# Weighted sums of a four-layer kernel: final products in quarters between the chunks, expansions in halves, and four batches in a loop body

## The chip, the cores and the metric

The kernel runs on one core of one Trainium2 chip. The metric is device time in microseconds (us) for one execution of the whole program. Five engines work side by side: TensorE (PE in the profile, with its weight loads as PEld), VectorE (DVE), ScalarE (ACT), GpSimd (POOL) and SyncE (SP), which here only issues transfers. Each works through its own instructions in order; they meet through semaphores.

## The reference, cut to what matters

Three attention layers run over 32 batches of 128 x 1024 numbers, and a fourth layer then aggregates over nearest neighbours. Only the last step of that fourth layer is touched:

```python
idx = _knn(x_loc, k)                     # k = 30 nearest of 1024 points
...
att = jax.nn.softmax(h[..., 0], axis=-1) # 1024 x 30 weights for each of 32 batches
xk = x.transpose(0, 2, 1)[bidx, idx]     # gathered rows
agg = jnp.einsum('bnkc,bnk->bnc', xk, att)
return x + agg.transpose(0, 2, 1)
```

So for each batch and each of 1024 points, 30 rows of 128 numbers are picked by index, weighted and summed, and `x` is added.

## The kernel before, in words

The kernel has four stages one behind the other: the attention layers and neighbour search over all batches (to about 5200 us), a small network with batch norms, the softmax, and the **weighted sums**, which is the stage of this change. It begins at about 5838 us and ends with the program.

In the weighted sums the gather is made into matrix products. A point's index is split into a low part l (0 to 15) and a high part h (0 to 63). For every batch `i`:

- **normalise** (DVE, line 1973) makes the attention weights of the batch; two **transposes** (PE, line 1111, tile TP) turn them.
- **weights** (DVE, line 1985, 16 instructions for each half of the batch) spread the turned weights over the 16 values of l, into BA (tile S for half 0, pd for half 1).
- **blocks** (ACT, line 1564, four instructions for each of four groups `v`), which this text calls expansions, spread BA into block form BD. There are two buffers of BD, one for even and one for odd `v`.
- **onehots** (DVE, line 1994, one instruction for each of eight chunks `c`) compare the high parts with 0 to 63, into A1 (tile gat, two buffers).
- **chunk** (PE, line 1124, 32 matmuls, each shown twice in the trace) multiplies A1 by BD into SCA (even `c`) or SCB (odd `c`). One BD serves two chunks.
- **columns** (ACT, line 1572, one instruction for each chunk) copy that result out into WT (two halves).
- **final** (PE, line 1137, 32 matmuls for each half, in pairs on PD and MISC that run together), the final product of WT with the table of rows X3D. The product of half 0 (the early one) needs chunks 0 to 3, that of half 1 (the late one) chunks 4 to 7. The late one is made inside the next batch's turn.
- **finish** (DVE, line 2008, two instructions), which the change calls the sums, adds `x` to both halves and lets the store go.

SP issues for each batch the store of the result, the load of the index table, of X3D and of `x`; these wait for finish. POOL splits the indices (lines 631 to 635).

The waits that matter: a chunk needs its one-hots, its BD, and the columns of the chunk two before it. The one-hots of chunk `c` need chunk `c - 2` done (buffer). The columns need their chunk. Expansions of `v` need both chunks of `v - 2` done. The early product needs finish of the batch before, since both products share the tiles PD and MISC. The order on each engine is written out by hand:

```python
# PE                                      # DVE                       # ACT, for v in range(4)
chunk 0, chunk 1                          normalise(i + 1)            blocks v + 1 (or 0 of i + 1)
final(i - 1, ..., 1)                      onehots 0, 1                columns 2v
transposes(i + 1)                         weights(i, 1)               columns 2v + 1
chunks 2 to 5                             onehots 2, 3
final(i, ..., 0)                          finish(i - 1)
chunks 6, 7                               onehots 4, 5
                                          weights(i + 1, 0)
                                          onehots 6, 7
```

PE and DVE run batch 0 as straight code, then a loop (`Fori`) of 15 passes with two batches in its body, then batch 31. ACT loops over 31 batches, one in its body. The loop bodies have 714 instructions on PE (a matmul counted once), 145 on DVE and 43 on ACT.

Of the kernel before, what the change touches and what calls it, by code (L numbers as in the profile page):

```python
# [31 lines left out]
def program(nc, x_in, ctx_in, mask_in, w_in, b_qkv, w_out, wq, wk, wv, wo, at, bq, bk, bv, bo,  # L32
            mlp_k, consts, out, NB=B):
# [16 lines left out]
    with stack:  # L50
# [195 lines left out]
        LV, HV = 16, 64  # L246
# [36 lines left out]
        def settle(eng):  # L283

            eng.sem_inc(waited, 1)
# [357 lines left out]
        def _(pe):  # L643
# [497 lines left out]

            def aggregate(i, par, k, first=False, last=False):
                chunk(i, 0)
                chunk(i, 1)
                if not first:
                    final(i - 1, 1 - par, k - 1 + par, 1)
                if not last:
                    transposes(i + 1, 1 - par)
                for c in range(2, 6):
                    chunk(i, c)  # L1150
                final(i, par, k, 0)
                chunk(i, 6)
                chunk(i, 7)
                if last:
                    final(i, par, k, 1)
# [13 lines left out]
        def _(act):  # L1169
# [388 lines left out]
            def blocks(i, v):  # L1558
                half, w = v // 2, v % 2
                act.wait_ge(ba_done, i * 2 + half + 5)  # L1560
                act.wait_ge(chunk_ready, i * 8 + 2 * v + 2)
                src = BA[half].rearrange("r (h p) l -> r h p l", h=2)[:, :, 32 * w:32 * w + 32, :]
                for j in range(4):
                    last = A(BD[v % 2][:, :, :, j, :], src, ACT.Copy, scale=blockmask[0:GROWS, j:j + 1])
                last.then_inc(bd_done, 1)
# [20 lines left out]
            blocks(0, 0)  # L1586
            with act.Fori(0, NB - 1) as i:
                aggregate(i)
# [4 lines left out]
        def _(dve):  # L1593
# [417 lines left out]
            def aggregate(i, par, k, first=False, last=False):  # L2011
# [26 lines left out]
            with dve.Fori(0, NB // 2 - 1) as pair:  # L2038
                for odd in (1, 0):
                    aggregate(pair * 2 + (2 - odd), odd, pair + (1 - odd))  # L2040
# [86 lines left out]
```

## Time and profile before

| | |
|---|---|
| time, median of 3 runs | 7017.76 us (6999.0 to 7027.35) |
| profiled execution, its own time | 6984.93 us |
| its span, first to last instruction | 6983.1 us |
| first chunk of the weighted sums | 5849.73 us |
| mean granted TensorE clock | 0.950 |
| PE busy over the whole span | 89% |
| DVE busy over the whole span | 87% |

The profile is of one execution. Its time exceeds its span by 1.8 us, and it is 32.8 us under the median of the runs, so a sum made on the trace is carried over to the median as a difference. Times of instructions below are microseconds from the start of the span. A bracket at the end of a row gives the idle time of that engine before the row and what ended it; "issue" means that nothing seen in the profile was waited for.

### The profile page before, as it was taken

The numbers are of one execution on the slowest core, as the hardware profiler recorded it, in microseconds if no ns is written. First come the engines' busy times: TensorE is split into PE (matmuls) and PEld (weight loads), VectorE is DVE, ScalarE is ACT, GpSimd is POOL, SyncE is SP. The second block draws the span as 40 slices with busy tenths as digits, with TensorE's granted clock in tenths as the row PEclk, the third lists the DMA queues.
The fourth block names the chain that finished last, engine by engine and source line by source line (L and its number), as shares of the span: only waits on it lengthen the run. The fifth ranks groups of instructions, "written<-read, shape, count | busy, mean of one in ns | idle before, by whom it ended". The sixth has DMA issues, their size and how long they took to land.

```text
span 6983.1 us, 208271 instructions
## 1 busy us (share of the span) xinstructions
PE 6195.4 (89%) x79430; PEld 4459.4 (64%) x79430; DVE 6047.0 (87%) x8509; ACT 4321.9 (62%) x10325; POOL 2693.2 (39%) x3399
## 2 busy tenths in 40 slices
PE   8999999999999999999999999999995795888888
PEld 4666666666666666666666666666664234888878
DVE  6999999989999999999999999999996578777776
ACT  4666666666666666666666666666662156666666
POOL 2444444454444444444444454444443101111110
PEclk9999999999999999999999999999997898999999
DMA  3222222222222222222222222222224003222222
GB/s 118 76 75 72 71 71 68 69 75 80 76 72 78 72 68 68 72 75 76 71 72 68 69 72 83 72 75 75 75 70 133 21 16 76 63 64 62 64 66 59
DMA packets 301388, 499.32 MB, mean 72 GB/s; under 512 B 103859, under 2 KB 217699, under 8 KB 299683
## 3 DMA queue, kind: packets, MB, share of 16 engines
q1 hardware_dynamic: 246733, 389.60, 18.3%
q10 hardware_dynamic: 53589, 95.21, 4.3%
q8 instruction: 706, 11.57, 0.7%
q14 instruction: 360, 2.94, 0.1%
HBM read 410.45 MB, written 74.30 MB: 69 GB/s over the span
## 4 chain that ended last, share of the span: by engine, by line
DVE 41%; PE 29%; issue 21%; DMA 5%; ACT 2%; DVEq 1%; SPq 0%; POOL 0%; ACTq 0%; POOLq 0%
DVE pd L1680 10%; DVE m L1670 9%; DVE idx L1676 8%; PE SCA L901 7%; PE PD L1137 6%; DVE mx L1692 4%; PE SCA L1124 3%; DMA gat<-low_scratch 3%; DVE gat L1624 3%; PE SCB L1124 3%; DVE gat L1994 2%; PE SCB L733 2%; PE SCA L1042 1%; PE SCB L1042 1%; PE TP L1050 1%
## 5 line engine op out<-in xcount | busy, mean ns | idle before, releaser
L1670 DVE MAX8 m<-pd 128x8 f32<-128x1024 f32 x1024 | 1244.3, 1220 | 154.5 <-issue 72.1
L1676 DVE FIND_INDEX8 idx<-m,pd 128x8 uint32<-128x1024 f32 x1024 | 1245.2, 1218 | 0.0
L529 POOL TENSOR_TENSOR prod<-prod,hm 128x480 f32<-128x480 f32 x384 | 396.2, 1032 | 1934.8 <-ACT prod L1310 1923.9
L1680 DVE MATCH_REPLACE8 pd<-m,pd 128x1024 f32<-128x1024 f32 x768 | 928.2, 1209 | 0.4
L1192 ACT ACTIVATE pd<-PD,xxcol 128x512 f32<-128x512 f32 x514 | 368.7, 717 | 722.3 <-PE PD L684 692.3
L708 PEld LDWEIGHTS MISC<-ptab,gat 128*128 128x128 bf16 x23400 | 642.3, 96 | 177.7 <-DVE gat L1624 87.7
L1994 DVE TENSOR_TENSOR gat<-maskT,con 120x2048 f32<-120x2048 f32 x256 | 584.0, 2322 | 166.8 <-PE SCA L1124 164.9
L708 PE MATMUL MISC<-ptab,gat 128*128 128x24 bf16 x23400 | 653.2, 174 | 80.8 <-DVE gat L1624 78.3
L1290 ACT ACTIVATE S<-SCA,mx 128x64 f32<-128x64 f32 (+1 forms) x2560 | 590.1, 406 | 118.7 <-DVE mx L1692 118.3
L1290 ACT ACTIVATE S<-SCB,mx 128x64 f32<-128x64 f32 (+1 forms) x2560 | 580.4, 387 | 19.9 <-DVE mx L1692 19.9
L683 PE MATMUL PD<-arena 128*128 128x512 f32 x1028 | 552.6, 619 | 33.0 <-ACT pd L1192 28.3
L1624 DVE TENSOR_SCALAR gat<-gat,con 128x2560 bf16<-128x2560 bf16 x396 | 427.7, 1086 | 82.6 <-DMA gat<-low_scratch 82.6
L631 POOL TENSOR_SCALAR maskT<-ctxT 120x256 f32<-120x256 f32 x32 | 12.9, 404 | 1241.1 <-DVE gat L1994 895.9
L797 PE MATMUL PD<-reg,arena 128*128 128x128 f32 x4096 | 488.1, 277 | 0.0
L901 PE MATMUL SCA<-arena,OT 128*128 128x512 f32 x1024 | 484.9, 634 | 0.0
L797 PEld LDWEIGHTS PD<-reg,arena 128*128 128x128 f32 x4096 | 467.1, 192 | 15.1 <-issue 12.3
L1243 ACT ACTIVATE kexp<-reg,con 128x256 f32<-128x256 f32 x1024 | 435.0, 521 | 10.8 <-PE SCA L833 8.7
L578 POOL TENSOR_SCALAR hm<-hif 128x240 bf16<-128x240 f32 x256 | 396.6, 1700 | 8.0
L872 PEld LDWEIGHTS TP<-reg,ET 128*64 128x64 f32 x8192 | 279.1, 137 | 179.2 <-issue 178.3
L1124 PE MATMUL SCA<-arena,gat 120*64 120x64 f32 x8192 | 281.4, 230 | 109.4 <-DVE gat L1994 81.6
L872 PE MATMUL TP<-reg,ET 128*64 128x34 f32 x8192 | 326.0, 226 | 57.8 <-DVE on L1704 56.9
L901 PEld LDWEIGHTS SCA<-arena,OT 128*128 128x128 f32 x1024 | 207.7, 207 | 251.4 <-issue 251.4
(272 smaller groups left out, 14188.3 us busy)
## 6 DMA issues: line engine op xcount, KB each, us to landing
gat<-low_scratch SPq DMA_DIRECT2D x396, 640.0 KB, 3.9
arena<-in_ctx ACTq DMA_DIRECT2D x33, 512.0 KB, 4.2
x_scratch<-arena ACTq DMA_DIRECT2D x33, 512.0 KB, 3.2
x3T_scratch<-reg ACTq DMA_DIRECT2D x33, 512.0 KB, 3.4
maskT<-in_mask SPq DMA_DIRECT2D x32, 512.0 KB
arena<-in_x ACTq DMA_DIRECT2D x32, 512.0 KB, 4.4
reg<-in_ctx ACTq DMA_DIRECT2D x32, 512.0 KB, 3.5
arena<-x3T_scratch SPq DMA_DIRECT2D x32, 512.0 KB, 6.0
```

What stands on the lines that cost most here:

```text
L683: mm(PD[:, :], ctx[:, t * P:(t + 1) * P], ctx[:, h * 512:(h + 1) * 512], start=True, stop=False)
L708: last = mm(place[:, o:o + 3 * NT], oh[n % NOH][:, kk * 256 + half * P:kk * 256 + (half + 1) * P], ptab[:, part, :, :].rearrange("p t c -> ...
L797: last = mm(PD[:, c % 2 * P:(c % 2 + 1) * P], Wq[:, kc, c * P:(c + 1) * P], hT[:, kc, :], start=(kc == 0), stop=(kc == KC - 1))
L872: last = mm(TP[64 * half:64 * half + 64, (4 * b + pair) * 2 * VW:(4 * b + pair + 1) * 2 * VW], ET[:, o:o + 64], V2[:, (4 * g + 2 * b + hal ...
L901: last = mm(SC[0][:, h * 512:(h + 1) * 512], OT[:, c * P:(c + 1) * P], Wo[:, c, h * 512:(h + 1) * 512], start=(c == 0), stop=(c == KC - 1))
L1124: last = mm(SC[c % 2][64 * h:64 * h + 64, p * 64:(p + 1) * 64], A1[c % 2][:, h, p, :], BD[v % 2][:, h, c % 2 * 16 + p, :, :].rearrange("r ...
L1290: last = A(S[g][:, r * keys:(r + 1) * keys], SC[g][:, r * keys:(r + 1) * keys], ACT.Exp, bias=mx[g][:, r:r + 1])
L1624: V.tensor_scalar(oh[n % NOH], oh[n % NOH], iota_p, None, ALU.is_equal).then_inc(oh_done, 1)
L1670: V.max(m, buf[:, :]).then_inc(found, 1)
L1676: last = V.max_index(idx[:, t, 8 * r:8 * r + 8], m, buf[:, :])
L1680: V.match_replace(buf[:, :], m, buf[:, :], -3.0e38).then_inc(found, 1)
L1994: V.tensor_tensor(A1[c % 2], low[:, :, 16 * part:16 * part + 16].unsqueeze(3) .broadcast_to([GROWS, 2, 16, HV]), iota64[0:GROWS, :].unsque ...
```

## The change

On PE each final product is cut into four quarters (four values of l each, 16 pieces in two lines of tiles), which are put between the chunks. On DVE finish goes from behind the fourth one-hots to behind the fifth, and weights of both halves each move earlier or later by a place. On ACT the expansions may be cut in halves, and only those of `v = 3` are really parted, by the columns of chunk 4; the expansions for the next batch stand behind the columns of chunk 5 instead of before those of chunk 6. All loops get four batches in their body: PE and DVE 7 passes over batches 2 to 29, ACT 7 passes over batches 0 to 27. The bodies then have 1426 instructions on PE, 285 on DVE and 163 on ACT. No computation is added or left out.

```diff
-            def final(i, par, k, half):
-                pe.wait_ge(wt_done, i * 8 + 4 * half + 6)
-                if half == 0:
-                    pe.wait_ge(x3T_ld[par], k * 32 + 32)
-                    pe.wait_ge(out_done, i + 2)
-                settle(pe)
-                for l in range(LV):
+            def final(i, par, k, half, piece):
+                if piece == 0:
+                    pe.wait_ge(wt_done, i * 8 + 4 * half + 6)
+                    if half == 0:
+                        pe.wait_ge(x3T_ld[par], k * 32 + 32)
+                        pe.wait_ge(out_done, i + 2)
+                    settle(pe)
+                for l in range(4 * piece, 4 * piece + 4):
...
-                last.then_inc(fin_ready, 1)
+                if piece == 3:
+                    last.then_inc(fin_ready, 1)
...
                 chunk(i, 0)
+                late(0)
+                late(1)
                 chunk(i, 1)
-                if not first:
-                    final(i - 1, 1 - par, k - 1 + par, 1)
+                chunk(i, 2)
+                late(2)
                 if not last:
                     transposes(i + 1, 1 - par)
-                for c in range(2, 6):
-                    chunk(i, c)
-                final(i, par, k, 0)
+                late(3)
+                chunk(i, 3)
+                chunk(i, 4)
+                final(i, par, k, 0, 0)
+                final(i, par, k, 0, 1)
+                chunk(i, 5)
                 chunk(i, 6)
+                final(i, par, k, 0, 2)
+                final(i, par, k, 0, 3)
                 chunk(i, 7)
...
-            with pe.Fori(0, NB // 2 - 1) as pair:
-                for odd in (1, 0):
-                    aggregate(pair * 2 + (2 - odd), odd, pair + (1 - odd))
+            aggregate(1, 1, 0)
+            with pe.Fori(0, (NB - 4) // 4) as four:
+                for u in range(4):
+                    aggregate(four * 4 + 2 + u, u % 2, four * 2 + 1 + u // 2)
+            aggregate(NB - 2, 0, NB // 2 - 1)
...
             def aggregate(i, last=False):
-                for v in range(4):
-                    if v < 3:
-                        blocks(i, v + 1)
-                    elif not last:
-                        blocks(i + 1, 0)
-                    columns(i, 2 * v)
-                    columns(i, 2 * v + 1)
+                for v in (1, 2):
+                    blocks(i, v, 0)
+                    blocks(i, v, 1)
+                    columns(i, 2 * v - 2)
+                    columns(i, 2 * v - 1)
+                blocks(i, 3, 0)
+                columns(i, 4)
+                blocks(i, 3, 1)
+                columns(i, 5)
+                if not last:
+                    blocks(i + 1, 0, 0)
+                    blocks(i + 1, 0, 1)
+                columns(i, 6)
+                columns(i, 7)
...
                 onehots(i, par, 0)
-                onehots(i, par, 1)
                 weights(i, par, 1)
-                onehots(i, par, 2)
-                onehots(i, par, 3)
+                for c in range(1, 5):
+                    onehots(i, par, c)
                 if not first:
                     finish(i - 1, 1 - par, k - 1 + par)
-                onehots(i, par, 4)
                 onehots(i, par, 5)
+                onehots(i, par, 6)
                 if not last:
                     weights(i + 1, 1 - par, 0)
-                onehots(i, par, 6)
                 onehots(i, par, 7)
```

How the instructions stand on the engines shows best in the last batch, whose code is straight. On VectorE, before, the last batch reads as follows (gat is A1, pd01 is BA of half 1, X1 and ET are the sums of batches 30 and 31):

```order
L1994 TENSOR_TENSOR gat<-maskT,con 120x2048 x2
L1985 SCALAR_TENSOR_TENSOR pd01<-maskT,TP 120x128 x16
L1994 TENSOR_TENSOR gat<-maskT,con 120x2048 x2
L2008 TENSOR_TENSOR X1<-PD,arena 128x8x64
L2008 TENSOR_TENSOR X1<-MISC,arena 128x8x64
L1994 TENSOR_TENSOR gat<-maskT,con 120x2048 x4
L2008 TENSOR_TENSOR ET<-PD,arena 128x8x64
L2008 TENSOR_TENSOR ET<-MISC,arena 128x8x64
```

And with the change, on the same engine, from the last one-hots of batch 30 on (the first row joins chunk 7 of batch 30 and chunk 0 of batch 31):

```order
L2023 TENSOR_TENSOR gat<-maskT,con 120x2048 x2
L2014 SCALAR_TENSOR_TENSOR pd01<-maskT,TP 120x128 x16
L2023 TENSOR_TENSOR gat<-maskT,con 120x2048 x4
L2037 TENSOR_TENSOR X1<-PD,arena 128x8x64
L2037 TENSOR_TENSOR X1<-MISC,arena 128x8x64
L2023 TENSOR_TENSOR gat<-maskT,con 120x2048 x3
L2037 TENSOR_TENSOR ET<-PD,arena 128x8x64
L2037 TENSOR_TENSOR ET<-MISC,arena 128x8x64
```

The sums of batch 30 moved behind four one-hots in a row (chunks 1 to 4) instead of behind two (chunks 2 and 3), and the weights of half 1 come before the one-hots of chunk 1.

On ScalarE, before, the last batch is this, from the expansions of `v = 1`:

```order
L1564 ACTIVATE arena<-S01,con 120x64x16 x4
L1572 ACTIVATE arena<-SCA 128x16x64
L1572 ACTIVATE arena<-SCB 128x16x64
L1564 ACTIVATE arena<-pd01,con 120x64x16 x4
L1572 ACTIVATE arena<-SCA 128x16x64
L1572 ACTIVATE arena<-SCB 128x16x64
L1564 ACTIVATE arena<-pd01,con 120x64x16 x4
L1572 ACTIVATE reg<-SCA 128x16x64
L1572 ACTIVATE reg<-SCB 128x16x64
```

With the change, ScalarE in the same batch, from the expansions of `v = 1`:

```order
L1581 ACTIVATE arena<-S01,con 120x64x16 x4
L1590 ACTIVATE arena<-SCA 128x16x64
L1590 ACTIVATE arena<-SCB 128x16x64
L1581 ACTIVATE arena<-pd01,con 120x64x16 x4
L1590 ACTIVATE arena<-SCA 128x16x64
L1590 ACTIVATE arena<-SCB 128x16x64
L1581 ACTIVATE arena<-pd01,con 120x64x16 x2
L1590 ACTIVATE reg<-SCA 128x16x64
L1581 ACTIVATE arena<-pd01,con 120x64x16 x2
L1590 ACTIVATE reg<-SCB 128x16x64
```

Only the last four expansions are parted, two before and two behind the columns of chunk 4.

On TensorE the last hunk of batch 0 shows the early product, before (-) and now (+); the rows left out are pieces on PD and MISC like those beside them:

```order
-L1124 MATMUL SCA<-arena,gat 64x64 x32
-L1124 MATMUL SCB<-arena,gat 64x64 x32
-L1137 MATMUL PD<-arena 128x256
-L1137 MATMUL MISC<-arena 128x256
...
+L1124 MATMUL SCB<-arena,gat 64x64 x32
+L1124 MATMUL SCA<-arena,gat 64x64 x32
+L1138 MATMUL PD<-arena 128x256
+L1138 MATMUL MISC<-arena 128x256
...
```

Before, all 32 pieces (line 1137) stand behind chunk 5 (SCB); now 16 of them (line 1138) stand behind chunk 4 (SCA), and 16 behind chunk 6 (SCA).

## Rows read from the trace of the kernel before

**Rows 1.** The page: span, busy time of each engine

```profile
span 6983.1 us, 208271 instructions
PE 6195.4 (89%) x79430; PEld 4459.4 (64%) x79430; DVE 6047.0 (87%) x8509; ACT 4321.9 (62%) x10325; POOL 2693.2 (39%) x3399
```

**Rows 2.** Timeline of PE, the transposes: start, duration, engine, line, tiles

```profile
5855.31 0.43 PE L1111 MATMUL TP<-con,OT 128*120 128x128 f32 x2
...
6315.41 0.43 PE L1111 MATMUL TP<-con,OT 128*120 128x128 f32 x2
...
6348.52 0.44 PE L1111 MATMUL TP<-con,OT 128*120 128x128 f32 x2
...
6385.16 0.43 PE L1111 MATMUL TP<-con,OT 128*120 128x128 f32 x2
...
6915.76 0.43 PE L1111 MATMUL TP<-con,OT 128*120 128x128 f32 x2
```

**Rows 3.** Timeline of PE over one batch, chunks 2 to 1

```profile
6315.78 2.08 PE L1124 MATMUL SCA<-arena,gat 120*64 120x64 f32 x64
6317.69 2.04 PE L1124 MATMUL SCB<-arena,gat 120*64 120x64 f32 x64
6320.65 2.09 PE L1124 MATMUL SCA<-arena,gat 120*64 120x64 f32 x64 [0.92 <-DVE gat L1994]
6322.76 2.08 PE L1124 MATMUL SCB<-arena,gat 120*64 120x64 f32 x64
6324.77 0.48 PE L1137 MATMUL PD<-arena,kexp 64*128 64x256 f32 x1
...
6325.31 0.38 PE L1137 MATMUL PD<-arena,kexp 64*128 64x256 f32 x1
...
6331.88 2.09 PE L1124 MATMUL SCA<-arena,gat 120*64 120x64 f32 x64
...
6336.76 2.08 PE L1124 MATMUL SCA<-arena,gat 120*64 120x64 f32 x64 [0.93 <-DVE gat L1994]
6339.40 2.08 PE L1124 MATMUL SCB<-arena,gat 120*64 120x64 f32 x64 [0.55 <-DVE gat L1994]
```

**Rows 4.** Timeline of DVE beside it: finish, one-hots, weights, normalise

```profile
6315.77 0.69 DVE L2008 TENSOR_TENSOR X<-PD,arena 128x512 f32<-128x512 f32 x1 [4.95 <-PE MISC L1137]
6316.37 0.68 DVE L2008 TENSOR_TENSOR X<-MISC,arena 128x512 f32<-128x512 f32 x1
6318.02 4.49 DVE L1994 TENSOR_TENSOR gat<-maskT,con 120x2048 f32<-120x2048 f32 x2 [0.97 <-PE SCA L1124]
6322.44 3.72 DVE L1985 SCALAR_TENSOR_TENSOR S<-maskT,TP 120x128 f32<-120x128 f32 x16
...
6330.39 0.40 DVE L1973 TENSOR_TENSOR OT<-arena,mb 128x240 f32 x1
```

**Rows 5.** Timeline of ACT beside it: columns, expansions

```profile
6317.91 1.02 ACT L1572 ACTIVATE arena<-SCA 128x1024 f32<-128x1024 f32 x1 [4.32 <-PE SCA L1124]
...
6320.70 4.26 ACT L1564 ACTIVATE arena<-pd,con 120x1024 f32<-120x1024 f32 x4
```

**Rows 6.** Timeline of PE around the loop's end

```profile
6005.17 0.48 PE L1137 MATMUL PD<-arena 64*128 64x256 f32 x1 [1.04 <-issue]
...
6011.60 2.04 PE L1124 MATMUL SCB<-arena,gat 120*64 120x64 f32 x64
6017.57 3.50 PE L1124 MATMUL SCA<-arena,gat 120*64 120x64 f32 x64 [3.94 <-issue]
```

**Rows 7.** Windows there: busy of engines, then PEclk, DMA share, GB/s

```profile
6003.00:6004.00 1.00, 1.00 (x11) 0.66 (x7) 1.00 (x1) 1.00 (x3) 0.00 (x0) 1.00 0.86 324
6013.00:6014.00 1.00, 0.64 (x22) 0.49 (x18) 1.00 (x1) 0.32 (x1) 0.00 (x0) 1.00 0.06 16
6018.00:6019.00 1.00, 1.00 (x25) 1.00 (x23) 1.00 (x7) 0.85 (x1) 0.00 (x0) 0.50 0.00 0
```

**Rows 8.** Waits of DVE from 600 to 5200 us, its main loop

```profile
DVE m L1670 <- issue: 65.1, 28, 2.5
```

More of the change, by code:

```diff
@@ L1139, in final, with late @@
                                   start=(l == 0), stop=(l == LV - 1))
-                last.then_inc(fin_ready, 1)
+                if piece == 3:
+                    last.then_inc(fin_ready, 1)
             def aggregate(i, par, k, first=False, last=False):
+                def late(piece):
+                    if not first:
+                        final(i - 1, 1 - par, k - 1 + par, 1, piece)
                 chunk(i, 0)
+                late(0)
+                late(1)
                 chunk(i, 1)
-                if not first:
-                    final(i - 1, 1 - par, k - 1 + par, 1)
+                chunk(i, 2)
+                late(2)
                 if not last:
                     transposes(i + 1, 1 - par)
-                for c in range(2, 6):
-                    chunk(i, c)
-                final(i, par, k, 0)
+                late(3)
[4 more added lines that the diff above has]
+                chunk(i, 5)
                 chunk(i, 6)
+                final(i, par, k, 0, 2)
+                final(i, par, k, 0, 3)
                 chunk(i, 7)
                 if last:
-                    final(i, par, k, 1)
+                    for piece in range(4):
+                        final(i, par, k, 1, piece)
             pe.sem_inc(attT_ready, 2)
@@ L1556, in _, with blocks @@
                 exponentials(q)
-            def blocks(i, v):
+            def blocks(i, v, part):
                 half, w = v // 2, v % 2
-                act.wait_ge(ba_done, i * 2 + half + 5)
-                act.wait_ge(chunk_ready, i * 8 + 2 * v + 2)
+                if part == 0:
+                    act.wait_ge(ba_done, i * 2 + half + 5)
+                    act.wait_ge(chunk_ready, i * 8 + 2 * v + 2)
                 src = BA[half].rearrange("r (h p) l -> r h p l", h=2)[:, :, 32 * w:32 * w + 32, :]
-                for j in range(4):
+                for j in (2 * part, 2 * part + 1):
                     last = A(BD[v % 2][:, :, :, j, :], src, ACT.Copy, scale=blockmask[0:GROWS, j:j + 1])
-                last.then_inc(bd_done, 1)
+                if part:
+                    last.then_inc(bd_done, 1)
             def columns(i, c):
@@ L1575, in aggregate @@
             def aggregate(i, last=False):
-                for v in range(4):
-                    if v < 3:
-                        blocks(i, v + 1)
-                    elif not last:
-                        blocks(i + 1, 0)
-                    columns(i, 2 * v)
-                    columns(i, 2 * v + 1)
+                for v in (1, 2):
[12 more added lines that the diff above has]
+                columns(i, 7)
             act.sem_inc(bd_done, 4)
             act.sem_inc(wt_done, 2)
-            blocks(0, 0)
-            with act.Fori(0, NB - 1) as i:
-                aggregate(i)
+            blocks(0, 0, 0)
+            blocks(0, 0, 1)
+            with act.Fori(0, NB // 4 - 1) as four:
+                for u in range(4):
+                    aggregate(four * 4 + u)
+            for u in range(3):
+                aggregate(NB - 4 + u)
             aggregate(NB - 1, last=True)
@@ L2037, in _ @@
             aggregate(0, 0, 0, first=True)
-            with dve.Fori(0, NB // 2 - 1) as pair:
-                for odd in (1, 0):
-                    aggregate(pair * 2 + (2 - odd), odd, pair + (1 - odd))
+            aggregate(1, 1, 0)
+            with dve.Fori(0, (NB - 4) // 4) as four:
+                for u in range(4):
+                    aggregate(four * 4 + 2 + u, u % 2, four * 2 + 1 + u // 2)
+            aggregate(NB - 2, 0, NB // 2 - 1)
             aggregate(NB - 1, 1, NB // 2 - 1, last=True)
```

## The prediction

> **What bounds the kernel now.** I first read the page's busy times [rows 1]: the kernel has 6983.1 us of span, PE 89% and DVE 87% busy, but that averages over four stages, and the change touches only the last. So next I took the timeline of PE in that stage. Each batch has one pair of transposes, so their starts mark the period. The first is at 5855.31 and the last, the 31st, at 6915.76: 30 periods in 1060.5 us [rows 2]. They are of two kinds. From 6315.41 to 6348.52 it is 33.11 us, from 6348.52 to 6385.16 36.64 us [rows 2]. The first kind recurs to within 0.1 us, the second comes every second batch, where PE's loop jumps back. Of the 30 periods one is the start (34.07 us), 15 are straight, 14 hold a jump: 1060.45 - 34.07 - 496.7 = 529.7 us, or 37.84 each, which is 4.73 us above a straight one.
>
> In a straight period PE has this to do, read from start to start [rows 3]. A chunk takes 6317.69 - 6315.78 = 1.91, say 1.92 us. An early product takes 6331.88 - 6324.77 = 7.11 us; from its evenly spaced pieces a quarter (8 steps of 0.2155 us) is 1.72 us, and 0.2 us goes at its two ends; the chunk ahead of a product takes 2.01 us (6324.77 - 6322.76), 0.1 more. So an uninterrupted group of quarters costs 1.72 us each plus 0.3. The transposes take 0.37 us. Eight chunks 15.36, eight quarters 13.79, two groups 0.6, transposes 0.37: **30.12 us**. The other 2.99 us of 33.11 are waits for one-hots: 1.05 ahead of chunk 4, 0.2 at chunk 5, 1.05 at chunk 0, 0.73 at chunk 1 [rows 3].
>
> Why they arise shows in DVE's row beside it [rows 4]. One-hots take 4.49 for two, 2.21 us each in a row, and start some 0.3 us after the end of the chunk that frees their buffer (chunk 2 starts 6315.78, DVE 6318.02). Before, PE makes four chunks in a row at 1.92, and DVE can't deliver at that pace through two buffers; then PE spends 7 us in a product while DVE idles (4.95 us ahead of finish [rows 4]). DVE's work in a batch is 8 x 2.21 + 2 x 3.6 + 0.4 + 1.3 = 26.6 us, ACT's is 4 x 4.16 + 8 x 0.92 = 24.0 us [rows 4, 5]. Neither is the bound; the order is.
>
> **The change, part by part.**
>
> *Quarters between chunks.* No more than two chunks now stand in a row. I lay the new order out with the durations above, t = 0 at the start of chunk 0. PE, if nothing is late: chunk 0 at 0, two late quarters 1.92, chunk 1 5.67, chunk 2 7.59, third quarter 9.51, transposes 11.53, fourth quarter 11.90, chunk 3 13.93, chunk 4 15.85, early quarters 17.77, chunk 5 21.51, chunk 6 23.43, early quarters 25.35, chunk 7 29.10, next chunk 0 31.02. There are five groups instead of two, so 3 x 0.3 = 0.9 us are added: 30.12 + 0.9 = **31.02 us**.
>
> *Is DVE in time?* Weights of half 1 end at 1.6, one-hots 1 at 3.8 (needed 5.67), 2 at 6.0 (7.59). Those of 3 wait for chunk 1 to end, 7.9 to 10.1 (13.93), 4 end 12.3 (15.85). Finish waits for the fourth late quarter, 14.3 to 15.6. One-hots 5: 16.2 to 18.4 (21.51), 6: 20.6 (23.43), weights of the next half 0: 24.2, one-hots 7: 26.4 (29.10), normalise 26.8, one-hots 0: 29.0 (31.02). Each is there 1.4 us or more ahead.
>
> *Is ACT in time?* Its columns start 0.2 us behind their chunk [rows 3, 5]. Columns 7 end 1.1 (late quarters need them at 1.92: the thinnest cover, 0.6 to 0.8 us), expansions 1 end 5.3, columns 0 6.2 (chunk 2 needs both at 7.59), columns 1 8.7, expansions 2 12.9, columns 2 13.8 (chunk 4, 15.85), columns 3 17.0 (early product, 17.77), first half of expansions 3 19.1, columns 4 20.0, second half 22.1 (chunk 6, 23.43). With all four in one piece columns 4 would end at 22.1, still in time, so the halving is worth nothing by itself; it is hidden by the early quarters. Columns 5 24.6, next expansions 0 28.7, columns 6 29.7 (31.02). Nothing waits, so a straight period falls by 33.11 - 31.02 = 2.09 us.
>
> *Finish one place later.* Finish follows the fourth late quarter at 14.3, and the early product needs it at 17.77; its 1.3 us are covered by chunks 3 and 4. The store and the loads behind it on SP start 3 us later in the batch; what they bring (rows of X3D) is needed a whole period on. Cost 0.
>
> *Four batches in a body.* PE makes 7 passes instead of 15, so 6 jumps instead of 14. A jump's price has three pieces. PE stands idle for 3.94 us between chunks 7 and 0 [rows 6]. After this idle time the clock is granted at 0.50, its level of 1.2 GHz [rows 7], and in this instance chunk 0 takes 3.50 instead of 2.08 us [rows 3, 6]; in others less. And within the early product of the batch ahead PE stops for about 1 us [rows 6], at the same matmul every time, with the DMA share still 0.86 in the microsecond before its stop [rows 7]. Together they are the 4.73 us. The 0.92 us wait for one-hots used to lie under the stop and is gone, so against the denser period a jump costs 4.73 + 0.92 = 5.65 us. Bounds: 4.4, if the stop within the product falls elsewhere, and 7 if clock and stop come fully each time. 6 x 5.65 = 33.9 us. DVE and ACT get longer bodies, 285 and 163 instructions against 145 and 43. Before, DVE goes from one-hots 7 into normalise without a gap across its jump; in its main loop, 337 instructions long, each jump costs 65.1 / 28 = 2.3 us [rows 8]. I take that for DVE, where it lies under PE's own stop (one-hots 0 would end 31.3, PE resumes at about 34.7), so 0. For ACT it falls between columns 7 and expansions 1, in the middle of PE's body, where expansions 1 and columns 0 have 1.3 us of cover: 2.3 - 1.3 = 1.0 us, six times, and since a body of 163 may also stay free of it I take half, 3 us (0 to 14).
>
> The Trainium skill ("Runtime: NRT & Kernel Launch", section on instruction fetch mechanics) says that instructions come in blocks of 16 KiB, 256 instructions, of which two are held, and that a taken branch out of these forces a fetch. The 16 GB/s in one microsecond of PE's stop [rows 7], that is 16 KB, agree with such a block. By that rule DVE's body of 285 must always pay at its jump; it is the third rival.
>
> *The sum.* 30 x 31.02 = 930.6, plus 33.9, plus 3, is 967.5 against 1060.5: -93. Behind the last transposes two products and chunks remain; the last batch has one more dense stretch, worth about 1.7 + 2 = 4 us. So **-97 us**. The profiled execution, 6984.9 us, would become 6888; its median lies 32.8 us higher, 7017.8 - 97 = **6921 us**.
>
> **The rivals.**
>
> *Fetches in the burst (0.14).* PE's instructions now run denser and are mixed differently. The stop within the early product [rows 6] came only where a fetch met the burst of loads. The burst follows finish and then lies over chunks 5 and 6, where instructions run out fastest. If each batch stops once for 1.4 us, 30 x 1.4 = 42 us come back: 6963 us. For it: the burst takes about 10 us in every batch. Against: before, it struck one batch in two only.
>
> *The waits move (0.10).* The list above leaves 0.6 to 1.4 us in several places. If DVE or ACT runs late and straight periods stay near 32.4, 30 x 1.4 = 42 us are lost, and half-way cases less: about 6960 us. For it: thin cover at columns 7. Against: DVE idles 4.4 and ACT 7 us in each batch.
>
> *Jumps on DVE and ACT at full price (0.10).* If ACT pays 2.3 us at each jump with no cover and DVE as much, 6 x 4.7 = 28 us: 6946 us.
>
> *Slower (0.04).* Finish now holds up everything behind it on DVE: one-hots 5 and 6, the next weights, through them expansions 0 on ACT, columns 6, and PE's chunk 0. That chain has 1.4 us of cover. If finish is late by x, the period grows by x - 1.4. It decides at (97 + 35) / 30 = 4.4 us a batch, so x = 5.8 us; then 7055 us. Finish has waited 4.95 us and less so far, and only for the product itself, so I see nothing that would do it.
>
> **How the numbers follow.** The forecast case has 0.62, the others as given. Its own bounds are 6905 (a jump at 4.4 us, ACT free: -10.5, groups at 0.2 us: -6) and 6935. The range goes on to the rivals at 6946 to 6963, and a little below: 6888 to 6966. About 0.5%, 35 us, is what a measurement of this kernel can tell from no change. Faster by more has the forecast and nearly all of the first three rivals, 0.90; within 0.5% 0.06; slower 0.04.
>
> **What would show it.** Straight periods between transposes near 31.0 us, PE's waits for one-hots [rows 3] nearly gone, six periods of 36 to 37 us, DVE idle ahead of finish about 2 us. Wrong: PE idle with "issue" inside chunks 5 and 6 (fetch), or PE waiting for ACT at the late quarters, chunk 2 or chunk 4.

## The result and the profile after

| | before | after |
|---|---|---|
| time, median | 7022.56 us (6999.0 to 7035.49) | 6898.14 us (6888.3 to 6909.3) |
| span of the profiled execution | 6983.1 us | 6900.7 us |
| first chunk of the weighted sums, to the end of the span | 1133.4 us | 1030.7 us |
| straight period | 33.11 us | 30.71 us |
| periods with a jump of PE's loop | 14, mean 37.84 us | 6, mean 36.15 us |

The ratio of the times is 0.9836, with a 95% interval from 0.981 to 0.9862: faster by 1.6%, clear of the noise, and by 124 us between the medians. Forecast were 97 us, 6921 us, in a range from 6888 to 6966.

The page of the changed kernel answers to [rows 1]:

```profile
span 6900.7 us, 208051 instructions
PE 6210.9 (90%) x79430; PEld 4447.3 (64%) x79430; DVE 6038.0 (87%) x8509; ACT 4318.0 (63%) x10325; POOL 2825.4 (41%) x3399
```

PE is as busy as before in microseconds and the span is 82 us shorter. The stage itself gained more, 1133.4 - 1030.7 = 102.7 us: in this execution it began at 5869.97 us and before at 5849.73, though nothing ahead of it was edited. Over the fourteen traces of this study that start lies between 5849.7 and 5895.8 us. So the medians' 124 us hold some 20 us that aren't shown to be the change's; the interval (97 to 133 us) holds the stage's 102.7. From here on kernels are compared by the stage, from the first chunk to the end of the span. Each stage time is that of one profiled execution, so a few microseconds between two kernels say nothing.

The timeline of PE, transposes, answers to [rows 2]: the first of 30 periods, a period with a jump (the two rows in the middle), and the last:

```profile
5880.03 0.43 PE L1111 MATMUL TP<-con,OT 128*120 128x128 f32 x2
...
6034.28 0.43 PE L1111 MATMUL TP<-con,OT 128*120 128x128 f32 x2
...
6071.24 0.43 PE L1111 MATMUL TP<-con,OT 128*120 128x128 f32 x2
...
6837.65 0.43 PE L1111 MATMUL TP<-con,OT 128*120 128x128 f32 x2
```

The 30 periods take 957.6 us against 1060.5. The jump one is 36.96 us. One straight batch on PE, answering to [rows 3], with the pieces of the products left out:

```profile
5972.47 0.43 PE L1111 MATMUL TP<-con,OT 128*120 128x128 f32 x2
...
5974.76 2.08 PE L1124 MATMUL SCB<-arena,gat 120*64 120x64 f32 x64
5976.68 2.04 PE L1124 MATMUL SCA<-arena,gat 120*64 120x64 f32 x64
...
5982.30 2.09 PE L1124 MATMUL SCB<-arena,gat 120*64 120x64 f32 x64
5984.21 2.04 PE L1124 MATMUL SCA<-arena,gat 120*64 120x64 f32 x64
...
5989.83 2.09 PE L1124 MATMUL SCB<-arena,gat 120*64 120x64 f32 x64
5991.75 2.04 PE L1124 MATMUL SCA<-arena,gat 120*64 120x64 f32 x64
...
5997.37 2.08 PE L1124 MATMUL SCB<-arena,gat 120*64 120x64 f32 x64
5999.28 2.04 PE L1124 MATMUL SCA<-arena,gat 120*64 120x64 f32 x64
...
6003.18 0.43 PE L1111 MATMUL TP<-con,OT 128*120 128x128 f32 x2
```

No row has a bracket: PE waits for nothing. The lists of PE's waits from 5900 to 6900 us say the same of all batches (us in total, times, longest). Two rows from before, then the only row for one-hots that is left:

```profile
PE SCA L1124 <- DVE gat L1994: 75.8, 52, 3.8
PE SCB L1124 <- DVE gat L1994: 7.8, 14, 0.6
...
PE SCA L1124 <- DVE gat L2023: 20.3, 6, 3.6
```

These six are the jumps of PE's loop. The chunks stand in pairs (3 and 4, 5 and 6, 7 and 0, 1 and 2), 1.92 us apart, and between the pairs lies half a product, 5976.68 to 5982.30, that is 5.62 - 1.92 = 3.70 us. DVE beside it, answering to [rows 4], now has its short pauses where the layout had them:

```profile
5975.13 0.69 DVE L2037 TENSOR_TENSOR X<-PD,arena 128x512 f32<-128x512 f32 x1 [1.73 <-PE MISC L1138]
5975.74 0.68 DVE L2037 TENSOR_TENSOR X<-MISC,arena 128x512 f32<-128x512 f32 x1
5977.01 4.49 DVE L2023 TENSOR_TENSOR gat<-maskT,con 120x2048 f32<-120x2048 f32 x2 [0.59 <-PE SCB L1124]
5981.42 3.72 DVE L2014 SCALAR_TENSOR_TENSOR S<-maskT,TP 120x128 f32<-120x128 f32 x16
...
5999.61 4.49 DVE L2023 TENSOR_TENSOR gat<-maskT,con 120x2048 f32<-120x2048 f32 x2 [1.90 <-PE SCB L1124]
```

Finish waits 1.73 us instead of 4.95, one-hots 5 wait 0.59 and one-hots 3 wait 1.90 us; the layout said about 2.0, 0.6 and 1.9. ACT, answering to [rows 5], has its parted expansions around columns 4:

```profile
5977.81 2.18 ACT L1581 ACTIVATE arena<-pd,con 120x1024 f32<-120x1024 f32 x2
5979.89 1.01 ACT L1590 ACTIVATE reg<-SCA 128x1024 f32<-128x1024 f32 x1
5980.80 2.18 ACT L1581 ACTIVATE arena<-pd,con 120x1024 f32<-120x1024 f32 x2
```

Around PE's jump, answering to [rows 6]: the small stop in the batch ahead and the large one.

```profile
6049.64 0.48 PE L1138 MATMUL MISC<-arena,kexp 64*128 64x256 f32 x1 [0.53 <-issue]
6052.64 2.09 PE L1124 MATMUL SCB<-arena,gat 120*64 120x64 f32 x64
6058.19 2.91 PE L1124 MATMUL SCA<-arena,gat 120*64 120x64 f32 x64 [3.46 <-DVE gat L2023]
```

The windows there, answering to [rows 7] (busy of the engines, then the clock, DMA share and GB/s):

```profile
6056.00:6057.00 1.00, 0.00 (x0) 0.00 (x0) 1.00 (x1) 1.00 (x2) 1.00 (x1) 1.00 0.00 0
6060.00:6061.00 1.00, 1.00 (x21) 0.91 (x17) 0.00 (x0) 0.00 (x0) 0.00 (x0) 0.50 0.00 0
```

PE is idle for 3.46 us, and then the clock is granted at 0.50 (1.2 GHz) as before. The releaser DVE in the bracket is the inferred kind: the one-hots it names were done at about 6051.5, when weights began. The clock doesn't fall behind every jump. At the fourth one it stays at its full level:

```profile
6446.14 2.08 PE L1124 MATMUL SCA<-arena,gat 120*64 120x64 f32 x64 [3.20 <-DVE gat L2023]
6447.00:6448.00 1.00, 1.00 (x42) 1.00 (x38) 0.00 (x0) 1.00 (x2) 0.00 (x0) 1.00 0.00 0
```

That is why the six periods with a jump differ: the two without a fall of the clock take 34.60 us, the four with one 36.5 to 37.4 us.

DVE's own jump lies between one-hots 7 of one batch and normalise at the head of its next turn:

```profile
6046.76 2.28 DVE L2023 TENSOR_TENSOR gat<-maskT,con 120x2048 f32<-120x2048 f32 x1
6048.96 0.39 DVE L2002 TENSOR_TENSOR OT<-arena,mb 128x240 f32 x1
6049.27 2.28 DVE L2023 TENSOR_TENSOR gat<-maskT,con 120x2048 f32<-120x2048 f32 x1
```

There is no pause there, although the body has 285 instructions; the 2.3 us of [rows 8] did not come.

### The profile page after: what moved, and what is told of

Read it like the earlier page. It is cut to its first block, busy times and chain, and to the rows that moved or that the text cites. A ratio compares the mean times of both kernels' runs of the same rounds, so it can differ in the third digit from the quotient of the medians.

```text
span 6900.7 us, 208051 instructions
## 1 busy us (share of the span) xinstructions
PE 6210.9 (90%) x79430; PEld 4447.3 (64%) x79430; DVE 6038.0 (87%) x8509; ACT 4318.0 (63%) x10325; POOL 2825.4 (41%) x3399
## 4 chain that ended last, share of the span: by engine, by line
DVE 39%; PE 32%; issue 20%; DMA 5%; ACT 2%; DVEq 1%; SPq 0%; POOL 0%; ACTq 0%; POOLq 0%
DVE pd L1709 9%; DVE m L1699 9%; DVE idx L1705 8%; PE SCA L901 7%; PE PD L1138 6%; PE SCB L1124 4%; DVE mx L1721 4%; PE SCA L1124 4%; DMA gat<-low_scratch 3%; DVE gat L1653 3%; PE SCB L733 2%; PE PD L683 1%; PE SCA L1042 1%; PE SCB L1042 1%; PE TP L1050 1%
## 5 line engine op out<-in xcount | busy, mean ns | idle before, releaser
L631 POOL TENSOR_SCALAR maskT<-ctxT 120x256 f32<-120x256 f32 x32 | 75.9, 2372 | 1013.5 <-DVE gat L2023 669.0
L1721 DVE TENSOR_REDUCE mx<-SCA 128x16 f32<-128x1024 f32 (+1 forms) x192 | 231.0, 1203 | 127.0 <-PE SCA L833 125.2
```

## The experiments

A table of the stage first, since the experiments answer each other. "Straight" is the period most batches have.

| kernel | stage, us | straight, us | jumps of PE, mean us |
|---|---|---|---|
| before | 1133.4 | 33.11 | 14, 37.84 |
| loops of the change only | 1140.9 | 33.1 to 33.6 | 6, 36.95 |
| order of the change only | 1060.7 | 30.71 | 14, 35.46 |
| the change | 1030.7 | 30.71 | 6, 36.15 |

### Which half of the change brings it

The first takes the kernel before and replaces only the loops, on PE as shown and likewise on DVE and ACT:

```diff
-            with pe.Fori(0, NB // 2 - 1) as pair:
-                for odd in (1, 0):
-                    aggregate(pair * 2 + (2 - odd), odd, pair + (1 - odd))
+            aggregate(1, 1, 0)
+            with pe.Fori(0, (NB - 4) // 4) as four:
+                for u in range(4):
+                    aggregate(four * 4 + 2 + u, u % 2, four * 2 + 1 + u // 2)
+            aggregate(NB - 2, 0, NB // 2 - 1)
```

> The order of before on all engines, only the loops of the changed kernel (four batches in a body on PE, DVE and ACT; 6 jumps instead of 14). The stage of weighted sums, from the first chunk to the end of the span, took 1133.4 us before and 1030.7 us with the whole change. If each jump of PE's loop costs its 4.73 us as read before, straight periods stay at 33.1 us and the stage falls by 8 x 4.73 = 38 us to about 1095 us. Rival: the order brings everything and what stops PE falls elsewhere in a longer body: 1125 us or more. Rival: longer bodies on ACT and DVE pay at their own jumps: 1095 plus up to 28 us.

The stage took 1140.9 us, and the time was 7027.84 us, ratio 0.9998 (0.9976 to 1.0019). My expectation missed by 46 us, and its first rival came: eight jumps fewer, and nothing gained. (That the stage is 7.5 us longer isn't shown to be the loops', by the ratio.) In groups of four the periods are about 33.5, then 34.3 to 37.1, 36.3 to 39.5, and 36.2 to 37.6 for the one with the jump. The timeline of PE in a fourth batch shows why, at the end of its chunk 5:

```profile
6187.61 0.33 PE L1124 MATMUL SCB<-arena,gat 120*64 120x64 f32 x3 [3.27 <-issue]
6187.88 0.79 PE L1137 MATMUL PD<-arena 64*128 64x256 f32 x1
```

61 of 64 pieces of the chunk were done, then PE stood for 3.27 us with nothing to wait for, and the product behind it began at half pace (0.79 us for its first piece instead of 0.48, 8.7 us in all instead of 7.1). The windows of that stretch:

```profile
6181.00:6182.00 1.00, 1.00 (x42) 1.00 (x39) 1.00 (x1) 1.00 (x2) 0.00 (x0) 1.00 1.23 223
6184.00:6185.00 1.00, 0.34 (x12) 0.20 (x8) 1.00 (x7) 1.00 (x2) 0.00 (x0) 1.00 1.37 203
6186.00:6187.00 1.00, 0.00 (x0) 0.00 (x0) 1.00 (x1) 0.00 (x0) 0.00 (x0) 1.00 0.66 250
6187.00:6188.00 1.00, 0.39 (x5) 0.32 (x5) 0.87 (x1) 0.02 (x1) 0.00 (x0) 0.91 0.05 20
```

The loads of X3D and x fill the DMA engines when PE stops (share over 1.2 from 6181 to 6185); it goes on when they have ended. The profile also lists the transfers of instructions, 16 KB each, as a queue of their own. Between 6175.5 and 6184.5 there is none, and from 6184.5 to 6186.1 there is one beside the loads (packets, MB, share of the DMA engines):

```profile
q8 instruction: 1, 0.02, 5.7%
```

It ran from 6184.57 to 6186.03, and PE went on 1.6 us after its end. The other stops look the same. Each of the 15 stops within a product before the change, and each of the 14 stops within a chunk or a product here, ends 1.3 to 1.6 us after the end of such a transfer. At the longest, 5.17 us at the end of a chunk 5, the transfer began only at 6618.94, 2.7 us after PE had stopped, as the loads ended. So what PE lacks there are instructions.

The second takes the changed kernel and puts the old loops back (two batches on PE, as shown, and on DVE, one on ACT):

```diff
-            aggregate(1, 1, 0)
-            with pe.Fori(0, (NB - 4) // 4) as four:
-                for u in range(4):
-                    aggregate(four * 4 + 2 + u, u % 2, four * 2 + 1 + u // 2)
-            aggregate(NB - 2, 0, NB // 2 - 1)
+            with pe.Fori(0, NB // 2 - 1) as pair:
+                for odd in (1, 0):
+                    aggregate(pair * 2 + (2 - odd), odd, pair + (1 - odd))
```

> The new order on all engines with the loops of before (two batches in a body on PE and DVE, one on ACT; 14 jumps). By the reading of the two traces a straight period is 30.7 us and one with a jump 36.15 us: 16 x 30.7 + 14 x 36.15 = 997 us for 30 periods against 979.6 with the whole change, plus what differs at the start, so the stage takes about 1030.7 + 8 x 5.4 = 1074 us. Rival: jumps cost less when they come oftener, because the clock or the fetch is caught up: 1050 us. Rival: the order needs the long bodies: straight periods above 31.5 us.

It took 1060.7 us, the time was 6940.52 us, ratio 0.9894 (0.9852 to 0.9937). The stage is 13 us shorter than expected, since straight periods are 30.71 us as foreseen but a jump costs 35.46 - 30.71 = 4.75 us and not 5.4: in this execution no product was stopped for more than 0.3 us, and behind 5 of the 14 jumps the clock didn't fall. So the order alone is worth 1133.4 - 1060.7 = 72.7 us, and the loops, given the new order, another 30.0. In the old order they are worth nothing. The two halves don't add up; the next experiment asks why.

### Do the stops come from the loads?

The first experiment's kernel, with the loads made small after batch 0. It leaves out the reload of most of X3D and of x, and is there for its time alone:

```diff
+                n, m = (LV, T) if full else (1, 128)
                 for h in range(2):
-                    sp.dma_start(X3D[par][64 * h:64 * h + 64, :, :],
-                                 table_dram[i, :, :].rearrange("(l h) c -> h l c", h=HV)).then_inc(x3T_ld[par], 16)
+                    sp.dma_start(X3D[par][64 * h:64 * h + 64, 0:n, :],
+                                 table_dram[i, :, :].rearrange("(l h) c -> h l c", h=HV)[:, 0:n, :]).then_inc(x3T_ld[par], 16)
...
-                sp.dma_start(x3b[par], x3_dram[i, :, :]).then_inc(x3_ld[par], 16)
+                sp.dma_start(x3b[par][:, 0:m], x3_dram[i, :, 0:m]).then_inc(x3_ld[par], 16)
```

> The first experiment (order of before, four batches in a body; its stage took 1140.9 us) with the loads of X3D and of x cut from 512 KB each to 64 KB each from batch 1 on, so that what goes out and comes in behind finish falls from about 1.6 MB to 0.8 MB a batch. It leaves out the reload of most of X3D and x, so its output isn't the reference's. In the first experiment PE stopped with issue for 1.4 us within an early product of the third batch and for 3.3 us plus 1.6 us around chunk 5 of the fourth, while the loads ran. If these stops come from instruction fetches that meet the loads, they vanish: periods are 33.1 us, jumps about 37, stage about 1090 us. Rival: they come from the length of the body alone: the stage stays at 1135 to 1141 us.

The stage took 1079.2 us, 61.7 less than with full loads, and 11 less than expected. (The text above has the sizes wrong: by the trace each load of X3D fell from 512 to 32 KB and that of x from 512 to 64 KB, so that with the store and the indices 2.2 MB a batch became 0.8 MB.) All stops inside the body are gone: batches without a jump take 33.10 us, and the six with one 34.6 to 36.2, mean 35.48. With the transfers of instructions seen above, this shows that the stops are fetches of instructions that come late behind the loads. The length of the body alone makes none.

It also splits the jump of the kernel before, if what it costs here may be carried over from a body of four batches to one of two: of the 4.73 us only 35.48 - 33.10 = 2.4 are the jump's. About 2.3 were the stop in the product [rows 6], the rest of what the loads cost, and the clock, which fell behind 11 of 14 jumps there and behind 3 of 6 here. Between periods with the same clock the loads cost 1.6 to 2.0 us.

That the jump costs so little in the old order has a second reason. PE's idle time at it is 3.2 to 3.6 us, much the same as in the new order (3.2 to 3.6), but it stands in place of the waits for one-hots at chunks 0 and 1 (0.93 and 0.55 us of idle time [rows 3]). The new order has no wait whose place it could take.

### Where the stops fall when nothing jumps

Straight code on PE for the old order (on top of the first experiment's kernel) and for the new order (on top of the changed kernel), the same edit:

```diff
-            aggregate(1, 1, 0)
-            with pe.Fori(0, (NB - 4) // 4) as four:
-                for u in range(4):
-                    aggregate(four * 4 + 2 + u, u % 2, four * 2 + 1 + u // 2)
-            aggregate(NB - 2, 0, NB // 2 - 1)
+            for i in range(1, NB - 1):
+                aggregate(i, i % 2, i // 2)
```

The old order:

> The order of before on all engines with straight code on PE and four batches in the bodies of DVE and ACT. No jump of PE is left. If fetches that meet the loads stop PE where the end of a block falls on chunk 5 or early in the product behind it, and the blocks' ends move by 34 instructions from batch to batch, then in each run of 7 or 8 batches two or three pay 1.4 to 4.5 us, the others take 33.1 us: stage about 1093 us. Rival: the stops of the first experiment belonged to the loop: all periods 33.1 us, stage 1066 us.

It took 1080.7 us (time 6961.9, one run), between the expectation (1093) and its rival (1066). Most periods are 32.92 us. Three in a row are longer, 33.76, 36.44, 36.07, and 13 batches on again three, 33.57, 37.75, 35.90. So the stops do move with the position of the code, but slower than I had thought: two groups in 30 periods, costing 16 us.

The new order:

> The changed kernel with all 32 batches as straight code on PE, loops of four on DVE and ACT. If the six long periods are PE's own jumps, they vanish, all 30 periods are 30.7 to 31.2 us, and the stage takes 1030.7 - 6 x 5.4 = 998 us. Rival: part of these 5.4 us belongs to the jumps of DVE, which stand at the same place: then periods of 32 to 34 us remain every fourth batch and the stage takes 1005 to 1020 us. Rival: straight code of this length meets fetch stops in many batches: 1020 us or more.

997.9 us, time 6880.55 us, ratio 0.9802 (0.9763 to 0.9841): the expectation met to 0.1 us. The six long periods were PE's jumps, and DVE's contribute nothing to them. Here too two groups of three periods stand out, 13 batches apart and three batches later than in the old order, but they are small: 31.21, 31.81, 31.77 and 31.39, 30.98, 32.29, together 5.2 us above 30.71 against 16 in the old order. Four stops within products go with them, and each ends 1.2 to 1.4 us after a transfer of instructions. The new order suffers a third as much from late fetches.

### The jumps of DVE and ACT

The changed kernel with two batches in DVE's body and one in ACT's:

```diff
-            with act.Fori(0, NB // 4 - 1) as four:
-                for u in range(4):
-                    aggregate(four * 4 + u)
-            for u in range(3):
-                aggregate(NB - 4 + u)
+            with act.Fori(0, NB - 1) as i:
+                aggregate(i)
```

> The changed kernel with two batches in DVE's body and one in ACT's, as before, and four in PE's. If the jumps of DVE and ACT lie under other work or cost nothing, the stage stays at 1031 us within 3 us. If ACT's jump in the middle of PE's body shows as the prediction priced it by halves (3 us, up to 14), the stage is shorter by that: 1017 to 1028 us. If a rule that a body longer than one block of 256 instructions always pays holds for DVE and is not covered, it is shorter too.

1030.5 us against 1030.7. Four batches in the bodies of DVE and ACT neither gain nor cost anything.

### The order on DVE and ACT

Three experiments each undo one thing of the new order in the changed kernel, and a fourth leaves PE's old. DVE's old order:

```diff
                 onehots(i, par, 0)
+                onehots(i, par, 1)
                 weights(i, par, 1)
-                for c in range(1, 5):
-                    onehots(i, par, c)
+                onehots(i, par, 2)
+                onehots(i, par, 3)
                 if not first:
                     finish(i - 1, 1 - par, k - 1 + par)
+                onehots(i, par, 4)
                 onehots(i, par, 5)
-                onehots(i, par, 6)
                 if not last:
                     weights(i + 1, 1 - par, 0)
+                onehots(i, par, 6)
                 onehots(i, par, 7)
```

> The changed kernel with the order of before on DVE alone (one-hots 0 and 1, weights, one-hots 2 and 3, finish, one-hots 4 and 5, weights, 6 and 7). Laid out with the durations of the trace, finish waits for the fourth late quarter, one-hots 4 come 2 us too late for chunk 4, and weights of half 1 and the one-hots around them are late too: a straight period is about 34.6 us, and the stage 1030.7 + 30 x 3.9 = 1148 us, so the quarters alone lose against before. Rival: DVE's reserve covers it, and the stage stays under 1060 us.

1144.5 us: all that the new order gained is lost, and the time of 7013.89 us is that of the kernel before (7011.32 in the same series). Most straight periods are 34.5 to 34.7 us, where the layout had 34.6; the one behind each jump is 35.9 us. The list of PE's waits from 5900 to 6900 us, where the change has 20.3 us in 6:

```profile
PE SCA L1124 <- DVE gat L2023: 86.9, 49, 3.3
```

Finish alone moved back, ahead of one-hots 4:

```diff
-                for c in range(1, 5):
+                for c in range(1, 4):
                     onehots(i, par, c)
                 if not first:
                     finish(i - 1, 1 - par, k - 1 + par)
+                onehots(i, par, 4)
                 onehots(i, par, 5)
```

> The changed kernel with finish one place earlier, behind the fourth one-hots instead of the fifth. By the layout finish waits for the fourth late quarter at 14.3 us, so one-hots 4 are ready at about 18 instead of 12.3 us, for chunk 4 due at 15.85: periods of about 33 us, stage 1030.7 + 30 x 2.2 = 1097 us. Rival: chunk 4 has cover elsewhere and it costs under 0.5 us a batch (stage under 1046 us).

1126.0 us, 95 more than the change; periods of 33.0 to 34.7 us, those with a jump 36.5 to 39.8. The expectation was 66 more. What it left out is the clock. Ahead of chunk 4 PE now waits about 2 us in every batch, and then two things happen, as in these two batches:

```profile
6119.24 2.08 PE L1124 MATMUL SCA<-arena,gat 120*64 120x64 f32 x64 [2.10 <-DVE gat L2023]
6120.00:6121.00 1.00, 1.00 (x42) 1.00 (x39) 1.00 (x1) 0.28 (x1) 0.00 (x0) 1.00 0.64 173
...
6152.16 3.13 PE L1124 MATMUL SCA<-arena,gat 120*64 120x64 f32 x64 [1.99 <-DVE gat L2023]
6153.00:6154.00 1.00, 1.00 (x24) 1.00 (x23) 1.00 (x1) 0.31 (x1) 0.00 (x0) 0.50 0.55 167
```

In the first the clock stays and the period is 33.03 us, as laid out; in the second it is granted at 0.50, the chunk takes 3.1 us instead of 2.1, and the period is 34.5 us. It fell behind 21 of the 31 such waits, and 21 x 1.5 us is about what the expectation missed. Placing finish is worth nearly all of the new order: it must not stand ahead of a one-hot that PE needs while its product is still being made.

The expansions in one piece:

```diff
                 blocks(i, 3, 0)
-                columns(i, 4)
                 blocks(i, 3, 1)
+                columns(i, 4)
                 columns(i, 5)
```

> The changed kernel with the expansions of the fourth group in one piece again, ahead of the columns of chunk 4. By the layout columns 4 then end at 22.1 us, for chunk 6 due at 23.4: no wait, the stage stays at 1031 us within 3 us. Rival: the columns of chunk 4 hold up chunk 6, since the measured period is 0.3 us shorter than laid out and the cover thinner: periods longer by 0.3 to 1 us, stage 1040 to 1060 us.

Straight periods stay at 30.71 us. The stage is 1037.0 us, 6 more, outside the 3 us expected but all in the six jump periods (37.2 us instead of 36.15 in the mean, 35.3 to 39.0). Those vary within one execution with the clock and with late fetches (34.2 to 37.3 in the second experiment), so nothing is shown that halving brings.

PE's old order, with the new one on DVE:

```diff
                 chunk(i, 0)
-                late(0)
-                late(1)
                 chunk(i, 1)
-                chunk(i, 2)
-                late(2)
+                for piece in range(4):
+                    late(piece)
                 if not last:
                     transposes(i + 1, 1 - par)
-                late(3)
...
```

> The changed kernel with the order of before on PE alone: whole products, four chunks in a row. DVE keeps its new order, with weights of half 1 between one-hots 0 and 1 and finish behind one-hots 4. Laid out with the durations of the trace a straight period is about 37 us, since four chunks in a row now wait for weights as well: stage 1030.7 + 30 x 6.5 = 1225 us. Rival: DVE's new order alone is as good with whole products: 1100 us or less.

1246.6 us, time 7109.21 us: the stage is slower by 113 us than before. The periods are 37.3 us with a jump and 38.7 to 39.9 us without, where the layout had 37: behind each of the 25 waits of about 3.6 us for one-hots the clock fell. The expectation of 1225 us had no such term. PE's order and DVE's fit only each other.

### A better version

The new order as straight code on PE, DVE and ACT:

> The new order with straight code on PE, DVE and ACT for all 32 batches (POOL and SP keep their loops). With PE alone straight the stage took 997.9 us. If the jumps of DVE and ACT lie under other work, it stays at 998 us within 3 us, and the time is about 6880 us, 0.980 of before. If they cost something by their meeting with loads it falls to 993 us.

999.2 us, time 6866.16 us, ratio 0.9817 (0.9799 to 0.9836); as with PE alone, so the jumps of DVE and ACT cost nothing here either. Then the transposes behind the fourth late quarter:

```diff
                 late(2)
+                late(3)
                 if not last:
                     transposes(i + 1, 1 - par)
-                late(3)
```

> The all-straight kernel with the transposes behind the fourth late quarter instead of between the third and the fourth, so that each product falls into two halves, not three pieces. With the transposes inside, the stretch from chunk 2 to chunk 3 takes 6.19 us (3.90 to the transposes, 2.29 on); without them between it would be 1.92 + 3.70 + 0.37 = 5.99 us. Straight periods go from 30.71 to 30.5 us, the stage from 999 to about 993 us. Rival: the break costs nothing and the period stays 30.7 us.

Straight periods are 30.51 us, the stage 990.7 us, the shortest of all, and the time 6865.53 us, ratio 0.9791 (0.9775 to 0.9807). Against the changed kernel that is 40 us less in the stage and 33 us between the medians; most of it is the straight code (1030.7 to 999.2), and the place of the transposes brings 0.20 us a batch. It also says that the quarters are not needed as such: with the transposes out of the way every product is made in two halves.

## Why the prediction was right, and where it wasn't

The time fell inside the range and the forecast case came, 27 us short of the medians' difference and 6 us short of what the stage shows (97 against 102.7). Step by step:

- **Waits for one-hots are the bound, and pairs with halves between them remove them.** Right. The straight period fell by 2.40 us instead of 2.09. The term that was too large was the ends of a group of quarters: I took 0.3 us for each of five; measured are 0.25 for each of the three undivided ones (3.70 - 3.45) and 0.45 for the one that the transposes part. That is the 0.31 us between 31.02 and 30.71.
- **DVE and ACT are in time, each by its place.** Right, and DVE's pauses agree within 0.3 us. DVE's old order costs 3.9 us a batch, as laid out.
- **Finish one place later costs nothing.** Right. Its old place costs 95 us in the new order on PE, about two thirds of them by the wait and the rest by the clock behind it.
- **Halving the expansions is worth nothing.** Nothing else was shown. My description of the change also said that the next batch's expansions moved; they stand behind columns 5 in both kernels.
- **A jump costs 5.65 us in the new order.** Measured 5.44. The step failed in another way: that the 4.73 us read from the kernel before belong to the jump, so that eight fewer save eight times that. In the old order eight fewer saved nothing. 2.4 us above a straight period were the jump's, the rest was the loads', and the stops move into other batches when the body changes. It came out right for the changed kernel because there a jump really costs about 5 us (4.75 with 14 of them, 5.44 with six) and late fetches are small. That the sum of 5.65 us is so near is partly luck: the stop of about 1 us within a product that it contained came at two of six jumps, as 0.53 and 0.28 us, and the idle time was 3.4 us in the mean instead of the 3.94 of the one instance read; against that, the wait of 0.55 us at chunk 1, too, no longer lies under the stop, and not only that of 0.92.
- **ACT pays at its jumps (3 us, 0 to 14), DVE 2.3 us each time under PE's stop.** Wrong, nothing: with the short bodies back the stage took 1030.5 us against 1030.7. I had read the Trainium skill ("Runtime: NRT & Kernel Launch", instruction fetch mechanics) as saying that DVE's body of 285 must leave the two blocks of 256 instructions that are held. It need not: it is shorter than two blocks, and the trace shows normalise following at once (6048.96 us, with no idle time before it).
- **The tail, 4 us.** From the last transposes to the end of the span 67.3 us before, 63.1 after: 4.3.

Of the rivals, the one with the fetches named a real mechanism with the wrong victim: late fetches struck hardest in the first experiment, in the old order. In the new order what is left of them is 0.2 to 0.5 us once in four batches. That the mixture of chunks and halves leaves more time for each fetch is the likely reason, since two chunks run through 256 matmuls and weight loads in 3.8 us and half a product through 64 in 3.7 us; shown is only that it suffers a third as much. What stays open is the 20 us by which the medians' difference exceeds the stage's, and why the clock falls behind some idle times and not behind others of the same length.

## What to carry to other kernels

When an engine waits for another in bursts, compare both engines' work per batch with the period: if neither fills it, lay out the order with durations from the trace and place the long piece of work so that no queue ahead of it stands still. Such an order holds for all engines together: PE's new order without DVE's gained nothing, and DVE's without PE's was 113 us slower than the kernel before. A layout made of durations gives the lower end where an engine is left waiting: behind waits of 2 us and more the clock cost another 1.5 us in most batches. And what a period with a loop's end takes longer is not wholly the loop's: before unrolling, see whether some of it is a stop that came while the DMA engines were full, for then it may only move.

## What the runs showed of the hardware

A dense stream of TensorE instructions (a chunk is 64 matmul and 64 weight load rows in 1.9 us) can be starved by data transfers. With the DMA share at 1.2 to 1.4 when it stopped, PE stood for up to 5.2 us in the middle of a chunk, and went on 1.2 to 1.6 us after a 16 KB transfer of instructions had ended; with the loads of X3D and x cut to 32 and 64 KB it never stopped there. At a jump of the loop PE stood for 3.2 to 3.9 us, and went on 1.8 to 2.0 us after such a transfer.

An idle time can also cost afterwards, since the clock may then be granted at 0.50 for a while: a product took 8.7 us instead of 7.1, a chunk 2.5 to 3.7 instead of 2.1. It fell behind 4 of the 6 jumps of the changed kernel, and behind 21 of 31 waits of about 2 us with finish early, but behind none of the 47 waits of 0.7 to 1.1 us for one-hots before the change.

The stage ahead of the change, untouched, began between 5849.7 and 5895.8 us, so effects of 20 us are better read in the trace of a stage than in the time of the whole.
